# One engine table, rewritten: statistics of x for units 3 to 6 in the lead, x by gate weights behind the mix, expert weights remade in pieces

## The chip, the cores and the metric

The kernel runs on one core of a Trainium2 chip. The metric is device time in microseconds (us) of one execution. Before the change it was 300.04 us, the median of three runs (297.88 to 300.93).

## The reference, cut to what matters

The input is a batch of 16 images of 16 by 16 positions with 128 channels, 4096 tokens in all. Two blocks follow each other, both with a residual.

```python
# block 1, per image (n = 256 tokens)
q = xn @ Wq + bq;  k = xn @ Wk + bk;  v = xn @ Wv + bv      # xn = layernorm of x, 64 columns each
maps = softmax(k, axis=tokens);  vectors = softmax(v, axis=tokens)
desc = einsum('bnd,bnv->bvd', q, maps)
x = x + einsum('bvd,bnv->bnd', desc, vectors) @ Wr + br
# block 2, per token, 8 experts, the best two
t = layernorm(x);  logits = t @ Wg;  w = softmax(top2(logits))
h = t @ W1[e];  g = t @ W3[e] + b3[e];  x = x + sum_e w_e * (silu(h) * g) @ W2[e]     # F = 384
```

## The kernel before, in words

The tokens are worked on in eight units of four 128-token pieces (two images each). A written-out table of steps -3 to 8 (`iteration`, one for each engine, with the same step number i) sets the order of each engine's instructions; nothing is scheduled at run time, each engine runs its list in order and waits on semaphores. Step i does the middle of unit i, the front of units i+1 (`new`) and i+2 (`later`), and the back of unit i-1 (`old`).

The work of a unit, in the order in which it depends on itself: `stats_of_x` and `add_eps` (VectorE, `BN_STATS` and `BN_AGGR`), `rough_rstd` (ScalarE, logarithm and exponential), `find_shift` (VectorE, a Newton step), `normalise_x` (ScalarE), `transpose_xn`, `copy_xnt`, `project_kv` (TensorE, ScalarE, TensorE), `max_kv` (VectorE), `exp_kv` (ScalarE), `invert_sums`, `normalise_probs`, `transpose_probs`, `copy_pk`, `weigh_tokens`, `copy_xk`, `mix_channels` (TensorE, 64 by 136), `add_mix_bias` (VectorE), `spread_br` and `attend` (TensorE), `add_logits`, `choose_pair`, `add_x`, `stats_of_x1`, `choose_experts` (VectorE), then, in the next step, `rank` (TensorE), `scale_gap`, `exp_gap`, `weigh_and_place` (VectorE), `normalise_t` (ScalarE) and eight indirect DMAs by GpSimd, `scatter_rows`, that write each token's row once for each of its two experts into `sorted_rows` in HBM. The logits of the second block are the product of normalised x with a centred gate weight, `logits_of_x` (TensorE, eight small matmuls), scaled on VectorE (`scale_x_logits`), plus a part that `attend` gives in extra columns.

The up weights (W1 and W3) must be centred over the input rows and their layernorm's last row replaced, since the rows are scattered with 127 normalised values and a constant 1 as the last. `remake_up(e)` does this on TensorE: a product of `elim` with the raw weights for each of W1 and W3, and a third product that adds expert e's b3 as the last row. ScalarE rounds the result to the high part (`round_weights`), VectorE subtracts it for the low part (`split_up`), and the banks are free for the expert after next only then. Two experts are remade in a step, from -1 to 3.

From step 4 on, sorted rows are read back in 71 tiles of 128 rows, each with one expert: `turn` on each engine, at the places of `TURNS`: tile -1 (preparation only) at place 1 of step 4, and eight a step from step 5. A turn is transpose, up (W1 and W3, high and low parts, six matmuls of 384 columns), activation, three transposes, down (six matmuls), and an indirect DMA by GpSimd into `result_rows`. The first tile waits for a table that VectorE computes in step 3 (`share_rows`, `fill_slots`) and for the scatters of units 1 and 2. In steps 0 to 3 `keep_busy` puts matmuls of ones, with no use for the result, on TensorE (four and three in a step).

Tiles 38 to 70 come behind the steps. At the end the sync queue reads the results back (`load_results`, 256 KB each, two halves for each of eight units): `wait_tiles` first takes sixteen counts from a table, one register load and one wait after another, for the early table and then, behind the ten loads of units 0 to 4, for the second (`first_half`, L508). VectorE adds the halves and ScalarE's queue stores them.

The sync queue (SP) is in order, too: it loads x, the raw weights, pads and then each tile's rows.

## Time and profile before

| | |
|---|---|
| median of 3 runs | 300.04 us |
| the profiled execution | 299.36 us, span 297.6 us |
| TensorE busy | 251.1 us (84% of the span) |
| ScalarE busy | 169.3 us (57%) |
| VectorE busy | 164.6 us (55%) |
| GpSimd busy | 133.7 us (45%) |
| DMA | 28.32 MB, mean 95 GB/s |

The shares are averages over three stages: a lead without tiles (to about 88 us), tiles beside unit steps and then alone (to about 283), and a tail of reading, adding and storing. TensorE's ends are modelled, so start to start is the better measure of a group's length.

### The profile page before, as it was taken

The page shows a single profiled execution, that of the slowest core. Times are in us where ns is not written, and L with a number is a line of the kernel's source. Part 1 is how long each engine was busy: PE and PEld are TensorE (multiplying, and loading weights), DVE is VectorE, ACT ScalarE, POOL GpSimd, SP SyncE. Part 2 cuts the span into 40 slices and gives each one's busy share as a digit, 9 for nine tenths or more (in the row PEclk, how much of TensorE's full clock was granted, in tenths as well). Part 3 has the DMA queues.
Part 4 walks back from the last instruction along what each step waited for, and adds up shares of the span by engine and source line. Part 5 has one row for each costly group of instructions (what it writes and reads, how often), then busy time and mean ns, then how long its engine had stood idle before and what let it go on. Part 6 is the DMA issues. An engine that isn't in the chain of part 4 may idle for free.

```text
span 297.6 us, 6603 instructions
## 1 busy us (share of the span) xinstructions
PE 251.1 (84%) x1602; PEld 208.7 (70%) x1602; DVE 164.6 (55%) x766; ACT 169.3 (57%) x484; POOL 133.7 (45%) x150
## 2 busy tenths in 40 slices
PE   8769897979839997989998896699998999999700
PEld 3435454645438986969897795689998999999600
DVE  4471868686764764485555448247533434343735
ACT  2635256657537679658756854775565565655400
POOL 4000006373721762773477377357763534444510
PEclk9657999997978999997999999999999999999975
DMA  4769301110112420112331011333333222147186
GB/s 124 257 208 326 88 0 37 36 45 29 48 43 58 116 65 19 47 53 73 90 85 62 29 55 54 83 92 89 109 101 89 57 61 77 46 142 269 33 273 238
DMA packets 31735, 28.32 MB, mean 95 GB/s; under 512 B 5146, under 2 KB 29540, under 8 KB 31700
## 3 DMA queue, kind: packets, MB, share of 16 engines
q1 hardware_dynamic: 24608, 16.82, 20.1%
q0 software_dynamic: 4320, 8.92, 8.9%
q10 hardware_dynamic: 2772, 2.17, 2.3%
q8 instruction: 15, 0.25, 0.4%
q14 instruction: 20, 0.16, 0.2%
HBM read 15.89 MB, written 12.01 MB: 94 GB/s over the span
## 4 chain that ended last, share of the span: by engine, by line
PE 55%; DVE 16%; issue 8%; ACT 8%; DMA 5%; SPq 4%; POOL 2%; DVEq 0%; ACTq 0%; POOLq 0%
PE bank L706 12%; PE bank L696 7%; PE bank L680 6%; PE bank L682 6%; PE bank L681 6%; PE bank L675 2%; SPq L508 2%; POOL sorted_rows L1460 2%; PE bank L613 2%; PE bank L568 2%; PE bank L622 2%; DMA both<-result_rows 1%; PE bank L585 1%; ACT row_buf L898 1%; DVE stats L1080 1%
## 5 line engine op out<-in xcount | busy, mean ns | idle before, releaser
L1460 POOL DMA_INDIRECT sorted_rows<-row_buf,position x64 | 61.6, 963 | 87.7 <-ACT row_buf L898 49.7
L1467 POOL DMA_INDIRECT result_rows<-ys,xs x71 | 68.4, 963 | 62.6 <-ACT ys L944 47.1
L1334 DVE TENSOR_TENSOR xs_lo<-bank,xs_hi 128x128 fp32r<-128x128 f32 x71 | 20.7, 291 | 80.3 <-ACT xs_hi L927 79.7
L706 PE MATMUL bank<-w_down,act_t 128*128 x426 | 60.0, 278 | 1.5 <-ACT act_t L937 1.5
L944 ACT ACTIVATE ys<-bank,xs 128x128 f32<-128x128 f32 x71 | 26.0, 367 | 59.0 <-PE bank L706 58.9
L706 PEld LDWEIGHTS bank<-w_down,act_t 128*128 128x128 f32 x426 | 53.8, 194 | 1.9 <-issue 1.9
L680 PE MATMUL bank<-w_up,xs_hi 128*128 x142 | 54.6, 385 | 0.0
L682 PE MATMUL bank<-w_up,xs_hi 128*128 x142 | 48.4, 341 | 0.0
L681 PE MATMUL bank<-w_up,xs_lo 128*128 x142 | 48.3, 340 | 0.0
L696 PE MATMUL bank<-ident,act_rows 128*128 128x128 f32 x213 | 35.9, 278 | 8.1 <-ACT act_t L937 6.1
L1341 DVE TENSOR_TENSOR act_rows<-silu_h,bank 128x384 f32<-128x384 f32 x71 | 38.9, 548 | 4.9 <-ACT silu_h L932 1.4
L932 ACT ACTIVATE silu_h<-bank 128x384 f32<-128x384 f32 x71 | 35.3, 497 | 5.7 <-PE bank L682 5.7
L696 PEld LDWEIGHTS bank<-ident,act_rows 128*128 128x128 f32 x213 | 25.8, 142 | 13.9 <-issue 9.5
L937 ACT ACTIVATE act_t<-bank 128x384 f32<-128x384 f32 x71 | 34.3, 483 | 0.0
L680 PEld LDWEIGHTS bank<-w_up,xs_hi 128*128 128x128 f32 x142 | 27.5, 193 | 0.0
L681 PEld LDWEIGHTS bank<-w_up,xs_lo 128*128 128x128 f32 x142 | 27.4, 193 | 0.0
L675 PE MATMUL bank<-ident,xs 128*128 128x128 f32 x71 | 20.3, 285 | 8.2 <-DVE xs_lo L1334 4.8
L682 PEld LDWEIGHTS bank<-w_up,xs_hi 128*128 128x128 f32 x142 | 27.1, 191 | 0.0
L927 ACT ACTIVATE xs_hi<-bank 128x128 fp32r<-128x128 f32 x71 | 19.8, 278 | 0.0
L675 PEld LDWEIGHTS bank<-ident,xs 128*128 128x128 f32 x71 | 10.5, 147 | 9.7 <-DVE xs_lo L1334 6.0
L898 ACT ACTIVATE row_buf<-x_all,shift,rstd 128x254 f32<-128x254 f32 x32 | 16.5, 594 | 0.0
L668 PE MATMUL bank<-all_ones 128*128 128x512 bf16 x42 | 15.2, 510 | 1.1 <-DVE all_ones L1029 1.1
(184 smaller groups left out, 347.6 us busy)
## 6 DMA issues: line engine op xcount, KB each, us to landing
xs<-sorted_rows SPq DMA_DIRECT2D x71, 65.0 KB, 1.9
both<-result_rows SPq DMA_DIRECT2D x16, 256.0 KB, 4.4
x_all<-x_dram SPq DMA_DIRECT2D x8, 256.0 KB, 3.5
out_dram<-both ACTq DMA_DIRECT2D x8, 256.0 KB, 2.6
both<-L_ffn_W_dram SPq DMA_DIRECT2D x2, 960.0 KB, 8.4
w_down<-L_ffn_W_dram SPq DMA_DIRECT2D x3, 512.0 KB, 10.3
both<-L_ffn_W_dram SPq DMA_DIRECT2D x2, 576.0 KB, 5.9
result_rows<-ys,xs POOLq DMA_INDIRECT x71, 2.3
```

The source lines that it names most:

```text
L675: nc.tensor.transpose(rows_t_of(s), xs[s.ring][:, 0:P], ident[:]).then_inc(xst_ps, 1)
L680: nc.tensor.matmul(o, xs_hi[s.par][:], w[0], start=True, stop=False)
L681: nc.tensor.matmul(o, xs_lo[s.par][:], w[0], start=False, stop=False)
L682: nc.tensor.matmul(o, xs_hi[s.par][:], w[1], start=False, stop=True).then_inc((h_ps, g_ps)[j], 1)
L696: last = nc.tensor.transpose(act_t_of(s)[:, k * P:(k + 1) * P], act_rows[s.par][:, k * P:(k + 1) * P], ident[:])
L706: last = nc.tensor.matmul(bank[4][:, 0:C], act_t[s.par][:, k * P:(k + 1) * P], w_down[:, ds(e, 1), k * C:(k + 1) * C].rearrange("p a c -> ...
L932: nc.scalar.activation(silu_h[s.par][:], h_of(s), ACT.Silu).then_inc(silu_ready, 1)
L937: nc.scalar.activation(act_t[s.par][:], act_t_of(s), ACT.Copy).then_inc(act_t_ready, 1)
L944: nc.scalar.activation(ys[s.n % RESULTS][:], bank[4][:, 0:C], ACT.Copy, scale=xs[s.ring][:, WEIGHT:WEIGHT + 1]).then_inc(y_sb, 1)
L1341: nc.vector.tensor_tensor(act_rows[s.par][:], silu_h[s.par][:], g_of(s), ALU.mult).then_inc(act_ready, 1)
L1460: nc.gpsimd.indirect_dma_start(out=sorted_rows.ap(), out_offset=bass.IndirectOffsetOnAxis(ap=position[u.par][:, c:c + 1], axis=0), in_=row ...
L1467: nc.gpsimd.indirect_dma_start(out=result_rows.ap(), out_offset=bass.IndirectOffsetOnAxis(ap=xs[s.ring][:].bitcast(I32)[:, DEST:DEST + 1], ...
```

## The change

It does five things.

- Statistics. `stats` and `mean_var` have a place for each unit, so the waits of `mean_var_read` go. The statistics of x of unit 3 move to step -1, those of units 4, 5 and 6 to step 0; steps 1 to 3 have none.
- The logits of x, and their scaling on VectorE, move behind the mix, in all steps.
- The bias b3 no longer goes through TensorE. ScalarE rounds it, VectorE takes the low part, and the sync queue copies the rows (16 transfers of 1.5 KB, two for each expert behind its `split_up`) into row 127 of the up weights. TensorE waits for them before tile -1.
- An expert is remade in two halves that stand apart; `round_weights` and `split_up` of the step's earlier expert come earlier; in steps -1 to 3 `transpose_probs` of the next unit stands at the end of a step instead of the start of the next. Fillers go from step 0 and eight come into step -2.
- The sync queue fetches all counts of a table before the waits, and those of the second table before the early loads.

The core of the diff (left out: declarations of the new semaphores and buffers, and the pieces for steps -2 and -1):

```diff
+            sp.wait_ge(b3_hi_ready, 1)
+            sp.wait_ge(b3_lo_ready, 1)
+            for e in range(E):
+                sp.wait_ge(up_lo_ready, e + 1)
+                for half, part in enumerate((b3_hi, b3_lo)):
+                    sp.dma_start(w_up[:].bitcast(F32)[P - 1:P, e, 1, half, :],
+                                 part[:].bitcast(F32)[e:e + 1, :]).then_inc(b3_rows_in, 16)
...
             sp.wait_ge(half_table, 1)
-            wait_tiles(early_half)
+            wait_tiles(counts_of(early_half))
+            first_counts = counts_of(first_half)
             for u in range(EARLY_UNITS):
                 for k in range(K):
                     load_results(Slot(u, LAST_RING, NU), k)
-            wait_tiles(first_half)
+            wait_tiles(first_counts)
...
-            def remake_up(e):
+            def remake_up(e, j):
+                if j == 0:
+                    pe.wait_ge(early_in if e < LOADED_FIRST else late_in, EXPERT_LOADS)
+                    pe.wait_ge(elim_ready, 1)
+                    at_least(pe, up_lo_ready, e - 1)
+                last = nc.tensor.matmul(up_banks(e)[j][:, 0:F], elim[:], w_raw[:, e, j, :], start=True, stop=True)
+                if j == 1:
+                    last.then_inc(up_ps, 1)
...
                 turn(slot_of_turn(i, 0))
-                if exists(i):
+                if exists(i) and i.n >= FIRST_STEP:
                     transpose_probs(i)
                 if exists(old):
                     rank(old)
-                if exists(new):
-                    logits_of_x(new)
...
-                if warm_up:
-                    at_least(pe, up_lo_ready, 2 * i.n)
+                    keep_busy(5, bank[4])
+                if middle is not None and i.n > 0:
+                    at_least(pe, up_lo_ready, middle - 1)
                     keep_busy(4)
+                    remake_up(middle, 0)
                 turn(slot_of_turn(i, 2))
                 if exists(i):
                     mix_channels(i)
-                if warm_up:
+                if exists(new):
+                    logits_of_x(new)
+                if middle is not None and i.n > 0:
                     keep_busy(3)
+                    remake_up(middle, 1)
...
-                if middle is not None:
-                    remake_up(middle)
                 turn(slot_of_turn(i, 5))
                 if exists(later):
                     transpose_xn(later)
+                if exists(new) and new.n < FIRST_STEP:
+                    transpose_probs(new)
+                if i.n == -2:
+                    keep_busy(3, bank[4])
+                if i.n == 0:
+                    for j in range(2):
+                        remake_up(middle, j)
+                elif end is not None and i.n > 0:
+                    remake_up(end, 0)
...
                 if end is not None:
-                    remake_up(end)
+                    remake_up(end, 1)
... ScalarE
                 turn(slot_of_turn(i, 0))
+                if has_norms(later) and i.n < FIRST_STEP:
+                    rough_rstd(later)
                 if exists(i):
                     copy_pk(i)
...
                     copy_xk(i)
+                if before is not None:
+                    round_weights(before)
                 turn(slot_of_turn(i, 2))
                 if exists(old):
                     normalise_t(old)
-                if before is not None:
-                    round_weights(before)
... VectorE
                 turn(slot_of_turn(i, 1))
+                if i.n == 0:
+                    stats_of_x(Step(0, 4))
                 if exists(new):
+                    invert_sums(new)
+                turn(slot_of_turn(i, 2))
+                if exists(old):
+                    weigh_and_place(old)
+                if i.n == 0:
+                    stats_of_x(Step(0, 5))
+                    stats_of_x(Step(0, 6))
...
                 if exists(i):
                     add_mix_bias(i)
+                if i.n != -1 and exists(new):
+                    scale_x_logits(new)
                 turn(slot_of_turn(i, 4))
-                if i.n != -1 and exists(i.shift(3)):
+                if i.n < -1 or i.n == 4:
                     stats_of_x(i.shift(3))
+                if before is not None:
+                    split_up(before)
...
-                for e in (before, middle):
-                    if e is not None:
-                        split_up(e)
+                if middle is not None:
+                    split_up(middle)
```

The order on TensorE in step 1, before (transposes of unit 1's probabilities, rank of unit 0, logits of x of unit 2, weigh, fillers, mix, fillers, attend, and then experts 3 and 4 with unit 3's transposes and projection between them):

```order
L622 MATMUL bank<-wg_mid,xn_t 128x8 x4
L585 MATMUL bank<-pk,xn 128x64 x4
L668 MATMUL bank<-all_ones 128x512 x4
L595 MATMUL bank<-wqr,xk 64x136 x2
L668 MATMUL bank<-all_ones 128x512 x3
L605 MATMUL bank<-br_parts,ones_row 128x272 x2
L613 MATMUL bank<-mix,probs 128x136 x4
L660 MATMUL bank<-both,elim 128x384
L661 MATMUL bank<-both,elim 128x384
L662 MATMUL bank<-b_in,b_row 128x384
L563 MATMUL bank<-ident,xn 128x128 x4
L568 MATMUL bank<-xn_t,wkv 128x512
```

The same place now:

```order
L597 MATMUL bank<-pk,xn 128x64 x4
L678 MATMUL bank<-all_ones 128x512 x4
L670 MATMUL bank<-both,elim 128x384
L607 MATMUL bank<-wqr,xk 64x136 x2
L634 MATMUL bank<-wg_mid,xn_t 128x8 x4
L678 MATMUL bank<-all_ones 128x512 x3
L670 MATMUL bank<-both,elim 128x384
L617 MATMUL bank<-br_parts,ones_row 128x272 x2
L625 MATMUL bank<-mix,probs 128x136 x4
L575 MATMUL bank<-ident,xn 128x128 x4
L588 MATMUL bank<-ident,probs 128x64 x4
L670 MATMUL bank<-both,elim 128x384
```

The logits (L622, now L634) went from the front to behind the mix, expert 3 from behind attend to before it, and no product with b3 is left.

VectorE in step 0, from the shift of unit 2's norm on, before:

```order
L1108 SCALAR_TENSOR_TENSOR shift<-mean_var,rstd 128x8
L1151 TENSOR_TENSOR x_logits<-bank,std_x 128x32
L1138 RECIPROCAL inv_sum<-exp_sum 128x2
L1122 TENSOR_TENSOR mix<-bank,bqr 64x272
L1069 BN_STATS stats<-x_all 128x6 x4
L1074 BN_AGGR mean_var<-stats 128x2 x4
L1161 TENSOR_TENSOR logits<-bank,x_logits 128x16 x2
```

And now, where the statistics of units 4, 5 and 6 stand in front of the bias of the mix:

```order
L1138 SCALAR_TENSOR_TENSOR shift<-mean_var,rstd 128x8
L1099 BN_STATS stats<-x_all 128x6 x4
L1104 BN_AGGR mean_var<-stats 128x2 x4
L1168 RECIPROCAL inv_sum<-exp_sum 128x2
L1099 BN_STATS stats<-x_all 128x6 x4
L1104 BN_AGGR mean_var<-stats 128x2 x4
L1099 BN_STATS stats<-x_all 128x6 x4
L1104 BN_AGGR mean_var<-stats 128x2 x4
L1152 TENSOR_TENSOR mix<-bank,bqr 64x272
L1181 TENSOR_TENSOR x_logits<-bank,std_x 128x32
L1229 TENSOR_TENSOR w_up<-bank,w_up 128x384 x2
L1191 TENSOR_TENSOR logits<-bank,x_logits 128x16 x2
```

The split of expert 0 (L1229) came in front of the logits; before, it stood at the end of the step with expert 1's.

## Rows read from the trace of the kernel before

**Rows 1.** The page's part 4: the chain that ended last, shares of the span.

```profile
PE 55%; DVE 16%; issue 8%; ACT 8%; DMA 5%; SPq 4%; POOL 2%; DVEq 0%; ACTq 0%; POOLq 0%
```

**Rows 2.** Windows by stage: busy us of each engine, granted clock, DMA share, GB/s.

```profile
107.00:132.00 25.00, 22.91 (x170) 20.69 (x169) 13.90 (x68) 19.23 (x53) 13.93 (x15) 1.00 0.12 39
```

**Rows 3.** Timeline of step 2: start, us, engine, line, operation, idle before and its releaser.

```profile
50.80 1.94 DVE L1199 TENSOR_TENSOR w_up<-bank,w_up 128x384 fp32r<-128x384 f32 x4
...
51.95 0.88 PE L660 MATMUL bank<-both,elim 128*128 128x384 f32 x2 [0.96 <-DVE w_up L1199]
...
52.65 0.68 DVE L1130 TENSOR_REDUCE neg_max<-bank 128x2 f32<-128x512 f32 x1
...
54.78 1.04 PE L622 MATMUL bank<-wg_mid,xn_t 128*128 128x8 f32 x8
...
55.50 0.17 DVE L1100 SCALAR_TENSOR_TENSOR newton<-var_eps,rough 128x8 f32<-128x8 f32 x1 [1.84 <-ACT rough L918]
...
55.67 1.08 PE L585 MATMUL bank<-pk,xn 128*128 128x64 f32 x8
...
56.79 0.28 ACT L891 ACTIVATE xk<-bank 128x128 f32<-128x128 f32 x1
...
57.55 0.68 PE L595 MATMUL bank<-wqr,xk 128*64 128x136 f32 x4
...
58.97 0.87 DVE L1069 BATCH_NORM_STATS2 stats<-x_all 128x6 f32<-128x128 f32 x4
...
59.17 1.19 PE L613 MATMUL bank<-mix,probs 64*128 64x136 f32 x8
...
60.43 0.26 DVE L1161 TENSOR_TENSOR logits<-bank,x_logits 128x16 f32<-128x16 f32 x2
...
64.90 1.94 DVE L1199 TENSOR_TENSOR w_up<-bank,w_up 128x384 fp32r<-128x384 f32 x4
```

**Rows 4.** Timeline of step 3 and the first tile.

```profile
71.07 2.06 ACT L898 ACTIVATE row_buf<-x_all,shift,rstd 128x254 f32<-128x254 f32 x4
...
83.39 1.94 DVE L1199 TENSOR_TENSOR w_up<-bank,w_up 128x384 fp32r<-128x384 f32 x4
...
88.07 0.45 PE L675 MATMUL bank<-ident,xs 128*128 128x128 f32 x1 [3.37 <-DMA xs<-sorted_rows]
```

**Rows 5.** The page's slices of 7.44 us: granted clock of TensorE in tenths.

```profile
PEclk9657999997978999997999999999999999999975
```

**Rows 6.** Windows, as rows 2: one microsecond of step 3.

```profile
71.00:72.00 1.00, 1.00 (x5) 0.22 (x4) 0.90 (x7) 1.00 (x3) 0.00 (x0) 0.67 0.00 0
```

**Rows 7.** Timeline of steps -2 to 0.

```profile
10.18 2.08 PE L568 MATMUL bank<-xn_t,wkv 128*128 128x512 f32 x2 [0.69 <-ACT xn_t L864]
...
17.11 0.91 ACT L878 ACTIVATE probs<-exps,inv_sum 128x256 f32<-128x256 f32 x2 [0.72 <-DVE inv_sum L1138]
...
20.09 0.30 ACT L850 ACTIVATE br_hi<-br_row 2x136 fp32r<-2x136 f32 x1
...
32.27 0.26 DVE L1161 TENSOR_TENSOR logits<-bank,x_logits 128x16 f32<-128x16 f32 x2 [0.54 <-PE bank L613]
```

**Rows 8.** Timeline, the start of step 5.

```profile
113.80 0.52 PE L696 MATMUL bank<-ident,act_rows 128*128 128x128 f32 x3 [1.55 <-ACT act_t L937]
```

**Rows 9.** Line L508: duration ns min/median/max, first and last start.

```profile
L508 SPq TENSOR_LOAD <-early_half x16: 263/267/274, 253.3 to 262.6; - x16
...
L508 SPq TENSOR_LOAD <-first_half x16: 261/270/809, 268.4 to 285.9; - x16
```

**Rows 10.** Chain of waits in the tail: start, us, what.

```profile
273.72 3.17 DMA result_rows<-ys,xs
...
289.71 4.45 DMA both<-result_rows
```

**Rows 11.** Timeline in the tail: last scatter, last loads of results.

```profile
283.80 1.04 POOL L1467 DMA_INDIRECT result_rows<-ys,xs  x1 [0.76 <-ACT ys L944]
...
286.57 3.60 SPq L502 DMA_DIRECT2D both<-result_rows  x6
```

88 lines of the change are left out of this document (46 added, 42 removed).

## The prediction

> **What bounds the kernel now.** I read the chain of waits first: TensorE carries 55% of it, VectorE 16%, and the sync queue 4% with one line, L508, that computes nothing [rows 1]. Then the windows by stage. From unit step 4 on, TensorE is busy 22.91 of 25 us at full clock [rows 2], so a tile starts when TensorE gets to it, and whatever the stage in front (the lead) saves reaches the end, less what is added to TensorE later. The three places to price are the lead, the tile steps 4 to 6, and the tail. All times are us from the span's start in the profiled execution: span 297.6, its own time 299.36, against a median of 300.04.
>
> **The lead, steps 1 to 3.** In the timeline of step 2 [rows 3] the reader is to see a ring: VectorE splits two experts (50.80), TensorE may then remake the next one (51.95, idle 0.96 before it), and only behind these matmuls stand the next transposes of probabilities, so that ScalarE's rough inverse and VectorE's Newton step come at 55.50, the copy of xk at 56.79, the mix at 57.55, attend at 59.17, the logits at 60.43 and the next split at 64.90. Split to split is 14.10. The change cuts the ring open: transposes and norms stand before the remaking, the bias matmuls are gone, the remade halves go between other work. The new ring, from the split: one expert only, half of 1.94, 0.97; maximum and bias of the next unit 1.0 (0.68 in its row and the short one behind it); from the Newton step to the end of the xk copy 1.57 (55.50 to 56.79 and its 0.28); 0.1 to the mix: 3.65. From mix to the end of attend it was 2.81 (57.55 to 59.17 + 1.19); now the logits of x, 0.89 (54.78 to the next start at 55.67), and one half of a remade expert, 0.75 (its row has 0.88, with a modelled end), stand in between: 4.45. From there to the next split VectorE does what it did, 4.54 (60.36 to 64.90). Together 12.64, so 1.46 less per step. TensorE's other work of a step (weigh, four fillers, a half in front of the mix; transposes, half, projection, half behind attend, some 3.5) still ends about 1 us before the ring closes. The statistics of x, 1.46 (58.97 to 60.43), leave VectorE in a stretch where it then waits for attend anyway, so they count nothing here; what they cost comes in step 0. For two rings, steps 1 and 2, I take **-2.8**, between -1.0 (a low clock for a few us) and -3.2.
>
> Step 3 hands over to the tiles through GpSimd: the first tile waits for the eight scatters of unit 2, which start after normalise_t [rows 4]. That was at 71.07, 6.17 behind the split at 64.90. Now it comes behind the xk copy (3.55) and one rounding of 0.85: 4.4. The scatters and the load until 88.07 are the same: **-1.75**. In front of the load stand sixteen small transfers of b3 rows on the same sync queue, the last two waiting for expert 7's split, which ended at 85.33 [rows 4]. One pair less before it and a ring without the low clock put it about 1 us before the last scatter lands; if it is late, that costs up to 1.0, and I keep that for the range.
>
> **The lead, steps -1 and 0.** This is the part with no row of its own. The first split and the first logits (32.27) hang on br_hi (20.09) [rows 7]. The probabilities come up to 2.9 earlier than 17.11, since their inverse stood behind statistics and waits; but the product that br_hi needs now follows the projection, and the projection took 2.08 at the low clock [rows 5, 7], so br_hi stays at about 20.1. Behind it VectorE now has split 0.9, b3's low part 0.4 (both estimates from instructions of like size), statistics of unit 3 1.46, maximum and bias 1.0, Newton 0.9, statistics of 4, 5 and 6 4.4, the mix bias 0.45, x logits and a split 1.1: 30.8 to 31.1 for the first logits, instead of 32.27. I take **-1.0**. One end is -2.4 (at full clock the projection, and so the product, would come about 1 us earlier, and the product itself is shorter); the other is +1.2, TensorE late with the remade experts 1 and 2 because step 0 has lost its seven fillers.
>
> **Tile steps 4 to 6.** The 0.89 of logits stood in step 4 in an idle stretch that lasts until 88.07 anyway [rows 4], and in step 5 inside ScalarE's block of two table loads, behind which TensorE idles 1.55 [rows 8]. Behind the mix there is nothing that they cover: TensorE idles 0.9 longer and then works 0.9 longer. Three steps of 0.89 are **+2.7**; the low end is 0, since the clock fell behind the stretch of small matmuls that they belong to, in step 3 [rows 6], and splitting it may avoid one.
>
> **The tail.** L508 loads a count and waits, sixteen times [rows 9]. After the result at 273.72 landed (3.17 later, 276.9), the queue spends until 286.57 on fifteen loads of 0.27 and what goes with them, and six loads of results go out together, the last from 289.71, landing 4.45 later [rows 10, 11]. The change fetches the counts earlier: they take 16 times some 0.5, 8, in front of the ten early loads, so those go out by about 275 (from 253.3: 9 for the early counts, 8, 5), just inside the 276.9. Then three loads leave at about 279, and the other three when the last result is in: the scatter at 283.80 plus the same 3.17 is 287.0 [rows 10, 11], the last load at 287.9. 289.71 less that is -1.8; fewer loads in flight may land a little faster. **-2.0**, from -1.0 to -3.1. The Trainium skill (DMA: Bandwidth & Descriptors, Latency and other measured facts) gives a register load a floor of some 600 ns; the rows have 0.27. By the page's figure sixteen would be 9.6, an estimate, and the early loads would end behind 276.9 by about an us.
>
> Counted at nothing: the buffers of statistics (memory only), the removed preparation of b3_row on VectorE (it stood beside waits), the fillers of step -2 (TensorE waited for ScalarE there).
>
> **Sum.** -2.8 - 1.75 - 1.0 + 2.7 - 2.0 = -4.85. 299.36 less that is 294.5; the median stood 0.7 above the profiled execution and I add half of it: **294.9**.
>
> **The rivals.** *A, the logits cost nothing*: for it, the low clock behind the small matmuls and the fact that TensorE must wait for ScalarE in each step; against it, TensorE is the bound there [rows 2]. 294.9 - 2.7 = 292.2. *B, the lead gives half*: step 0 starts TensorE cold, VectorE's statistics hold back the mix, and the queue is late with b3: +1.2 instead of -1.0 at the start, -1.4 instead of -2.8 for the rings, 0.6 for the queue; 294.9 + 4.2 = 299.1. *C, slower*: the clock. The rows show that it falls within a microsecond in which TensorE was busy throughout (a mean of 0.67, so from 2.4 to 1.2 GHz in the middle of it) [rows 6], and at 10.18 it was at the lower level, where the projection took 2.08. Now nothing fills step 0, and TensorE waits there for VectorE's mix bias for several us. A ring wholly at 1.2 GHz takes up to 4.45 more, from mix to attend. Two such rings are 8.9, and the time is 303.8. It decides from little more than one of them: 300.04 less 294.9 is 5.1. Against it: between about 30 and 82 us the page shows the clock low in one stretch only [rows 5], and the new ring keeps its seven fillers. The Trainium skill (TensorE: Matmul & The Clock Gate, The HAM clock gate) says that "the default state is throttled, and activity releases the throttle"; that speaks for C in step 0, while the row at 71 us shows a fall without an idle stretch, which the sentence alone would not give. *D, the tail does nothing*, since the queue is late or the landing is set by other traffic: 294.9 + 2.0 = 296.9.
>
> **Chances.** Forecast 0.50, A 0.17, B 0.13, D 0.12, C 0.08. A measurement of this kernel tells about 1% (3 us) from no change, so faster means below 297.0. The forecast's own range, from the ends above, is 292 to 297.5; with A whole and most of B and D, 8 in 10 lie in 291.0 to 298.6. Faster: forecast 0.44, A 0.17, D 0.07, B 0.02: 0.70. Same: forecast 0.06, D 0.05, B 0.10, C in a mild form 0.02: 0.23. Slower: C 0.06, B 0.01: 0.07.
>
> **What would show it.** The step from split to split at 12.6 (if 14, the ring is not cut); the first logits of unit 0 near 31; the first tile's transpose about 5.5 earlier than 88.07; an idle of 2.4 instead of 1.55 before the act transposes of step 5; the six late loads of results in two groups of three, the first before 280. A granted clock of 0.5 over more than 3 us in steps 1 to 3 makes it wrong upwards; a distance from first tile to last matmul that has not grown by 2 to 3 us makes it wrong downwards.

## The result, and the profile after

The changed kernel takes **297.01 us** (median of 19 executions, 296.01 to 300.89) beside 300.40 for the kernel before on the same chips (19 executions, 297.60 to 303.12). The ratio is 0.994, 95% interval 0.991 to 0.997: 0.6% faster, about 1.8 us, less than the 1% that the prediction took as what can be told, and far from its 1.7% (5.1 us). The median lies in the forecast's range of 292 to 297.5; the forecast itself, 294.9, is below every execution.

The ratio compares undisturbed executions only, which is why it is nearer to one than the two medians are.

The profiled execution is one of the longer ones, 300.29 us, with a span of 298.5 against 297.6 before. It has to be read piece by piece. First the page: what bounds the kernel is what it was [rows 1], except that the sync queue's 4% has gone to 1%:

```profile
PE 57%; DVE 15%; ACT 10%; issue 8%; DMA 5%; POOL 2%; SPq 1%; DVEq 0%; ACTq 0%; POOLq 0%
```

**The start.** VectorE and TensorE in steps -1 and 0, the rows that answer to [rows 7] (start, us, engine, line, operation):

```profile
15.76 2.07 PE L580 MATMUL bank<-xn_t,wkv 128*128 128x512 f32 x2
...
24.77 0.79 PE L607 MATMUL bank<-wqr,xk 128*64 128x136 f32 x4 [2.02 <-ACT xk L914]
...
26.81 0.84 DVE L1099 BATCH_NORM_STATS2 stats<-x_all 128x6 f32<-128x128 f32 x4
28.20 0.45 DVE L1152 TENSOR_TENSOR mix<-bank,bqr 64x272 f32<-64x272 f32 x1
28.68 0.19 DVE L1181 TENSOR_TENSOR x_logits<-bank,std_x 128x32 f32<-128x32 f32 x1
28.79 1.01 DVE L1229 TENSOR_TENSOR w_up<-bank,w_up 128x384 fp32r<-128x384 f32 x2
...
29.68 2.17 PE L625 MATMUL bank<-mix,probs 64*128 64x136 f32 x8
...
31.89 0.26 DVE L1191 TENSOR_TENSOR logits<-bank,x_logits 128x16 f32<-128x16 f32 x2 [2.09 <-PE bank L625]
...
36.92 1.02 DVE L1229 TENSOR_TENSOR w_up<-bank,w_up 128x384 fp32r<-128x384 f32 x2 [0.53 <-ACT w_up L931]
```

The kernel before, in the same places (mix on TensorE, mix bias, first full split on VectorE):

```profile
28.62 1.17 PE L595 MATMUL bank<-wqr,xk 128*64 128x136 f32 x4
...
29.83 0.45 DVE L1122 TENSOR_TENSOR mix<-bank,bqr 64x272 f32<-64x272 f32 x1 [2.85 <-PE bank L595]
...
36.71 1.95 DVE L1199 TENSOR_TENSOR w_up<-bank,w_up 128x384 fp32r<-128x384 f32 x4
```

The mix comes at 24.77, nearly four us earlier than before. Most of that is lost behind it. VectorE has three statistics in front of the mix bias, which comes at 28.20, only 1.6 earlier. VectorE then finishes expert 0's split at 29.80 and idles 2.09 until attend is done: attend takes 2.17, where later steps have 1.19. From mix bias to logits it is 3.69, where it was 2.44. So the logits come at 31.89, 0.4 earlier than 32.27, and the split that starts the first ring at 36.92, 0.2 *later* than 36.71. The forecast had 1.0 earlier.

**The rings.** The splits of steps 2 and 3 on VectorE, which answer to [rows 3]:

```profile
49.40 1.01 DVE L1229 TENSOR_TENSOR w_up<-bank,w_up 128x384 fp32r<-128x384 f32 x2
...
61.58 1.01 DVE L1229 TENSOR_TENSOR w_up<-bank,w_up 128x384 fp32r<-128x384 f32 x2
```

36.92, 49.40, 61.58: rings of 12.48 and 12.18 where they were 14.09 and 14.10. From there the first tile's transpose, at 82.63 by the next row, comes 21.05 later, where it was 23.17 [rows 4].

```profile
82.63 0.45 PE L685 MATMUL bank<-ident,xs 128*128 128x128 f32 x1 [5.59 <-DMA xs<-sorted_rows]
```

The lead is 5.44 shorter; 5.55 was forecast. That the sum agrees is luck: the rings and the hand-over gave 1.1 more, the start 1.2 less. The prediction also named a sign for being wrong upwards, a granted clock of 0.5 over more than 3 us in steps 1 to 3. It came, from 73 to 86.6 us, behind the step's last projection and over the first tile; TensorE had little to do there, and the hand-over was not longer for it.

**Step 5.** TensorE's timeline, the rows that answer to [rows 8]:

```profile
105.73 1.00 PE L597 MATMUL bank<-pk,xn 128*128 128x64 f32 x8
109.18 0.52 PE L706 MATMUL bank<-ident,act_rows 128*128 128x128 f32 x3 [2.44 <-ACT act_t L964]
```

Windows over the same stretch (length, busy time of PE, PEld, DVE, ACT, POOL with the number of instructions, then the granted clock, DMA share, GB/s):

```profile
106.00:108.00 2.00, 0.73 (x7) 0.60 (x6) 0.63 (x5) 1.78 (x6) 0.00 (x0) 1.00 0.00 0
108.00:110.00 2.00, 0.82 (x8) 0.85 (x9) 0.39 (x2) 1.74 (x6) 0.20 (x1) 1.00 0.01 4
110.00:112.00 2.00, 2.00 (x11) 1.74 (x9) 0.44 (x2) 1.43 (x5) 1.20 (x2) 0.64 0.10 33
112.00:114.00 2.00, 2.00 (x9) 1.47 (x8) 1.82 (x10) 1.93 (x4) 0.52 (x1) 0.50 0.10 33
114.00:116.00 2.00, 2.00 (x11) 2.00 (x11) 0.42 (x3) 0.00 (x0) 0.73 (x1) 0.50 0.00 0
...
120.00:122.00 2.00, 2.00 (x13) 2.00 (x13) 0.61 (x2) 1.45 (x5) 1.54 (x2) 0.80 0.13 44
```

The idle time is 2.44 where it was 1.55, as forecast (2.4). Behind it the clock falls from 1.00 to 0.50 (from 2.4 to 1.2 GHz) and stays there until 121 us, with TensorE busy throughout. The number of instructions per window shows the price: 9 to 11 in 2 us, where [rows 2] has 170 in 25, 13.6 in 2.

**The tail.** The chain of waits (start, us, what), the rows that answer to [rows 10]:

```profile
285.53 3.31 DMA result_rows<-ys,xs
...
288.98 0.36 SPq L510
289.39 0.73 SPq L510
290.16 4.94 DMA both<-result_rows
```

The sync queue's register loads (duration in ns, first and last start), which answer to [rows 9]:

```profile
L514 SPq TENSOR_LOAD <-early_half x16: 261/266/287, 255.0 to 263.3; - x16
L514 SPq TENSOR_LOAD <-first_half x16: 261/268/358, 265.4 to 273.7; - x16
```

The register loads no longer stand in the late wait, and the chain goes through the last scatter instead. From that scatter to the last load's issue it is now 290.16 - 285.53 = 4.63, where it was 289.71 - 283.80 = 5.91 [rows 10, 11]: 1.3 saved. But the load takes 4.94 instead of 4.45.

The six late loads do leave in two groups of three, but the first group at 281.3 to 284.7 and not before 280: the sixteen counts hold up the ten early loads, which begin at 274.3, when those of the kernel before (from 263.2) had just landed. The early loads themselves are down by 286.3 and do not reach the last ones. What they push back is what hangs on them, the stores of the five early units: their last one landed at 288.9 before, 0.8 ahead of the last load's issue, and lands at 293.7 now, 3.5 behind it. The DMA queues from 290 to 293.7 us (q10 has the stores, q1 the loads; packets, MB, share of the 16 engines):

```profile
q10 hardware_dynamic: 602, 0.57, 60.5%
q1 hardware_dynamic: 558, 0.54, 41.7%
```

In the kernel before, from 289.7 to 294.2 us, q1 is alone:

```profile
q1 hardware_dynamic: 1187, 1.13, 74.0%
```

### The profile page after: what moved, and what is told of

It reads as the page before. It is cut to its first block, busy times and chain, and to the rows that moved or that the text cites. A ratio compares the mean times of both kernels' runs of the same rounds, so it can differ in the third digit from the quotient of the medians.

```text
span 298.5 us, 6585 instructions
## 1 busy us (share of the span) xinstructions
PE 245.3 (82%) x1587; PEld 210.4 (70%) x1587; DVE 164.1 (55%) x765; ACT 169.9 (57%) x485; POOL 133.8 (45%) x150
## 3 DMA queue, kind: packets, MB, share of 16 engines
q10 hardware_dynamic: 2772, 2.17, 2.4%
## 4 chain that ended last, share of the span: by engine, by line
PE 57%; DVE 15%; ACT 10%; issue 8%; DMA 5%; POOL 2%; SPq 1%; DVEq 0%; ACTq 0%; POOLq 0%
PE bank L716 14%; PE bank L706 7%; PE bank L692 7%; PE bank L690 7%; PE bank L691 7%; PE bank L625 3%; PE bank L685 3%; POOL sorted_rows L1504 2%; PE bank L634 2%; PE bank L670 2%; ACT act_t L964 2%; ACT L998 2%; DMA both<-result_rows 2%; PE bank L607 1%; DVE stats L1099 1%
## 5 line engine op out<-in xcount | busy, mean ns | idle before, releaser
L716 PEld LDWEIGHTS bank<-w_down,act_t 128*128 128x128 f32 x426 | 54.4, 196 | 1.9 <-issue 1.9
L690 PE MATMUL bank<-w_up,xs_hi 128*128 x142 | 55.0, 387 | 0.0
L692 PE MATMUL bank<-w_up,xs_hi 128*128 x142 | 49.1, 346 | 0.0
L691 PE MATMUL bank<-w_up,xs_lo 128*128 x142 | 48.9, 344 | 0.0
L1376 DVE TENSOR_TENSOR act_rows<-silu_h,bank 128x384 f32<-128x384 f32 x71 | 39.0, 549 | 4.8 <-ACT silu_h L959 1.4
L706 PEld LDWEIGHTS bank<-ident,act_rows 128*128 128x128 f32 x213 | 26.4, 144 | 16.3 <-issue 10.9
L954 ACT ACTIVATE xs_hi<-bank 128x128 fp32r<-128x128 f32 x71 | 19.7, 277 | 2.1 <-PE bank L685 2.1
L670 PE MATMUL bank<-both,elim 128*128 128x384 f32 x32 | 15.2, 579 | 0.0
```

The costliest lines, as they stand in the source:

```text
L690: nc.tensor.matmul(o, xs_hi[s.par][:], w[0], start=True, stop=False)
L691: nc.tensor.matmul(o, xs_lo[s.par][:], w[0], start=False, stop=False)
L692: nc.tensor.matmul(o, xs_hi[s.par][:], w[1], start=False, stop=True).then_inc((h_ps, g_ps)[j], 1)
L706: last = nc.tensor.transpose(act_t_of(s)[:, k * P:(k + 1) * P], act_rows[s.par][:, k * P:(k + 1) * P], ident[:])
L716: last = nc.tensor.matmul(bank[4][:, 0:C], act_t[s.par][:, k * P:(k + 1) * P], w_down[:, ds(e, 1), k * C:(k + 1) * C].rearrange("p a c -> ...
L1376: nc.vector.tensor_tensor(act_rows[s.par][:], silu_h[s.par][:], g_of(s), ALU.mult).then_inc(act_ready, 1)
```

## The experiments

A common ruler makes the profiles comparable: the start of VectorE's gated rows (the product that writes act_rows, L1376; L1341 in the kernel before) of each of the 71 tiles, less that of the kernel before (92.23 for tile 0, 278.04 for tile 70). Where the difference changes, something was lost or won in that place. Step 4 ends with tile 1, step 5 has its logits at tile 9, step 6 at tile 17, step 7's idle time is ahead of tile 24. "Tail" is the span less the start of tile 70; it was 19.56. "Filled" and "products nobody reads" mean matmuls of ones on TensorE whose result is not used.

| run | tile 0 | tile 1 | tile 8 | tile 9 | tile 16 | tile 17 | tile 23 | tile 25 | tile 70 | tail | median us | ratio to before |
|---|---|---|---|---|---|---|---|---|---|---|---|---|
| the changed kernel | -5.33 | -4.69 | -4.22 | -0.30 | +0.57 | +1.26 | +1.31 | +1.32 | +1.73 | 18.73 | 297.01 | 0.994 |
| after_again | -4.35 | -3.30 | -3.22 | -2.55 | -2.75 | -2.05 | -1.98 | -0.63 | -0.10 | 19.06 | 297.32 | 0.995 |
| logits_front | -4.42 | -4.19 | -4.20 | -4.20 | -4.29 | -4.29 | -4.28 | -2.77 | -2.40 | 19.16 | 295.55 | 0.986 |
| fill_holes | -5.17 | -4.38 | -4.34 | -3.65 | -3.89 | -3.20 | -3.16 | -1.81 | -1.58 | 17.84 | 297.06 | 0.994 |
| before_behind | +0.23 | +1.25 | +1.29 | +1.97 | +1.79 | +2.47 | +2.50 | +3.86 | +4.21 | 19.35 | 305.22 | 1.020 |
| lead_only | -4.10 | -3.84 | -3.78 | -3.79 | -3.86 | -3.86 | -3.76 | -2.24 | -1.95 | 19.71 | 297.54 | 0.990 |
| tail_only | +4.37 | +4.41 | +4.41 | +4.41 | +4.37 | +4.38 | +4.38 | +5.82 | +5.72 | 18.64 | 299.17 | 0.995 |
| front_fill | -5.42 | -5.45 | -5.42 | -5.42 | -4.31 | -4.30 | -4.20 | -4.19 | -2.94 | 18.10 | 293.48 | 0.980 |
| front_first | -6.09 | -6.08 | -6.08 | -6.08 | -6.15 | -6.14 | -6.05 | -4.53 | -4.22 | 18.48 | 296.11 | 0.981 |
| best | -6.21 | -6.20 | -6.20 | -6.20 | -6.27 | -6.26 | -6.16 | -6.14 | -5.77 | 17.53 | 292.15 | 0.978 |
| best_stats | -5.94 | -5.93 | -5.93 | -5.93 | -5.01 | -5.01 | -4.89 | -4.87 | -3.72 | 18.38 | 292.49 | 0.978 |
| best_start | -8.12 | -8.11 | -8.07 | -8.07 | -8.14 | -8.13 | -8.05 | -8.03 | -7.74 | 18.00 | 289.88 | 0.970 |
| before_again | +0.14 | +0.14 | +0.14 | +0.13 | +0.15 | +0.16 | +0.15 | +0.17 | +0.23 | 19.23 | (one run: 299.24) | |
| after_start | -7.32 | -6.23 | -6.16 | -5.48 | -5.70 | -5.01 | -4.93 | -3.57 | -3.39 | 18.45 | 295.33 | 0.987 |
| best_twelve | -11.39 | -11.38 | -11.33 | -11.33 | -10.43 | -10.43 | -10.35 | -10.33 | -9.14 | 17.80 | 288.78 | 0.966 |

The 95% intervals of the ratios reach 0.003 to 0.007 to either side, for front_first 0.011. Four series were measured on four chips, with the kernel before beside each (medians 300.42 for the runs up to before_behind, 300.99 from lead_only to front_first, 302.08 from best to before_again, 299.49 for the last two), so across series the ratios are the better comparison.

**after_again**, the changed kernel unchanged.

> The changed kernel unchanged, beside the others on one chip. Its first profile (300.29 us) shows TensorE's clock at 0.50 from 112 to 120 us, in step 5, and its other times lie in two groups: 296.0 to 297.4 us where the mean granted clock is 0.920 or more, 298.8 to 300.9 us where it is 0.914 or less. Theory 1 (the holes): the low stretch in step 5 is what tells the groups apart. This profile then either shows the stretch again and a time near 300, or none there and a time near 296.5. Rival 2 (chance elsewhere): the slow group has its loss in another place each time, and a profile near 296.5 us can show the stretch in step 5 all the same. Median by both 296.5 to 298.

The profile gave neither outcome of theory 1: an execution of 298.78 us (span 297.0) with no low stretch in step 5. The median, 297.32, is in the range of both. Windows over the same idle time (2.44 again):

```profile
108.00:110.00 2.00, 0.13 (x2) 0.00 (x0) 0.13 (x1) 1.81 (x4) 0.00 (x0) 1.00 0.00 0
110.00:112.00 2.00, 1.43 (x12) 1.46 (x13) 0.83 (x3) 1.35 (x6) 0.81 (x1) 1.00 0.01 4
112.00:114.00 2.00, 2.00 (x15) 1.56 (x13) 0.84 (x4) 2.00 (x7) 1.11 (x2) 1.00 0.10 33
```

It lost 1.0 in the lead and 1.4 behind step 7's idle time instead. So the long stretch in step 5 is one form of a loss that comes in several places, as rival 2 has it.

**logits_front**, the logits of steps 4 to 6 where the kernel before has them (the same on VectorE for their scaling):

```diff
                 if exists(old):
                     rank(old)
+                if exists(new) and i.n >= FIRST_STEP:
+                    logits_of_x(new)
...
                 if exists(i):
                     mix_channels(i)
-                if exists(new):
+                if exists(new) and i.n < FIRST_STEP:
                     logits_of_x(new)
```

> The changed kernel with the logits of x (L634) of steps 4 to 6 back ahead of the first slot of the step on TensorE, and their scaling back on VectorE; the lead is left as changed. Theory 1: with the logits behind the mix TensorE idles 2.44 us in step 5 ahead of the act transposes, instead of 1.55, and the clock falls behind that hole in a part of the executions, which costs 3.9 to 4.5 us each time. With the logits in front the hole is 1.4 to 1.6 us, no stretch at 0.50 follows it, and the slow group is gone or rare: median 294.5 to 295.5 us (295.4 is the lower group's 296.4 less the 0.9 us of idle time). Rival 2: the logits' place is without effect on the clock and hides in the hole anyway: 296 to 298 us, with a low stretch in step 5 or 6 in as many executions as before.

295.55, the ratio 0.986 where the changed kernel's on the same chip is 0.995: the move costs the changed kernel about 2.6 us (1.8 by the two medians). The ruler shows it as the forecast had it, a fixed price per step without any fall of the clock: +0.67 from tile 8 to 9 and +0.70 from 16 to 17 in after_again, 0.00 and 0.00 here; step 4 costs 1.05 there and 0.23 here. The idle time in step 5 is back at 1.53. Rival 2, that the place costs nothing, is out.

**fill_holes**, products nobody reads ahead of the weighing of steps 5 and 6:

```diff
                 pe.wait_ge(pk_sb, u.n + 1)
+                for _ in range(FILL.get(u.n, 0)):       # FILL = {5: 20, 6: 12}
+                    nc.tensor.matmul(bank[1][:, 0:2 * P].rearrange("p (a b) -> p a b", a=2), all_ones[:],
+                                     all_ones[:].unsqueeze(1).broadcast_to([P, 2, P]), start=True, stop=True)
```

> The changed kernel with products nobody reads (256 columns each, 20 in step 5 and 12 in step 6) on TensorE ahead of the tokens' weighing, where it idled 2.44 us in step 5 and 1.4 in step 6. Theory 1: the idle time before the act transposes of step 5 falls below 0.5 us, nothing else is delayed by more than 0.3 us, and the clock stays at 1.00 through steps 5 and 6: median 296.0 to 296.8 us and no execution over 298. Rival 2: a fall comes anyway, in steps 5 to 6, since it is not set off by this hole: two groups as before, median 296.5 to 298. Rival 3 (it is the load itself, not the hole, that brings the clock down): the added work makes falls more frequent and the median 299 or more.

The idle time was filled (0.24 left), the steps 5 and 6 ran at 1.00, and the median is the changed kernel's. Theory 1 in its strong form, that the hole in step 5 makes the changed kernel's spread, has fallen: four of the twelve executions are over 298, one of them at 300.41, and the profile has its fall in step 7.

**before_behind**, the kernel before with the logits behind the mix in steps 4 to 6 alone (the edit of logits_front the other way round).

> The kernel before with one part of the change: the logits of x behind the mix in steps 4 to 6. Theory 1: the hole in step 5 grows from 1.55 to 2.4 us, so this is 0.9 us slower with nothing else, and in executions whose clock falls behind that hole another 4 us: median 1 to 4 us above the kernel before. Rival 2: at most 0.9 us slower, with no more low stretches than the kernel before. The prediction had +2.7 us for this part.

2.0% slower. Again +1.0, +0.68 and +0.68 at tiles 1, 9 and 17, 2.4 together, then 1.36 behind step 7's idle time, where this execution's clock fell and the two profiles of the kernel before have none. The ratio stands for 5.9 us, with an interval of 3.9 to 8.0, more than the 2.4 and a fall; the profiled execution, 303.42, is one of the faster of the six. What the rest is, is not shown.

**lead_only** and **tail_only** take the parts one by one. lead_only is logits_front with the old wait for the second table at the tail:

```diff
             wait_tiles(counts_of(early_half))
-            first_counts = counts_of(first_half)
...
-            wait_tiles(first_counts)
+            for b in range(RING):
+                count = sp.value_load(first_half[0:1, b:b + 1], min_val=16, max_val=16 * ((NS + RING - 1) // RING))
+                wait_in_front(sp, waited_sp, (y_out[b], count))
```

> The changed kernel with the logits of x of steps 4 to 6 in front again and with the counts of the last wait read where the kernel before reads them, so that the lead alone is changed. The run with the logits in front and the tail changed gave a median of 295.55 us and a ratio of 0.986 to the kernel before. Theory A (the tail is worth what the traces show between the last tile and the last load's start, 1.1 to 1.7 us, less 0.5 to 0.8 us that the last load then takes longer): 0.4 to 1.2 us slower than that run, 296.0 to 296.8 us. Rival B (the tail's forecast, 2.0 us, holds in most executions): 297.5 us. Against the kernel before, Theory A gives the lead 3.5 to 4.5 us of gain, the forecast had 5.55.

tail_only puts the new fetching of counts, for both tables, into the kernel before.

> The kernel before with the tail's part of the change alone: the counts of the last wait are loaded into SyncE's registers ahead of the first results' loads. From the last tile's gated rows to the start of the last load the kernel before took 11.67 us and the changed kernel 10.0 to 10.5. Theory A: the same 1.2 to 1.7 us here up to the load's start and a load 0.3 to 0.8 us longer than 4.45 us, 0.4 to 1.2 us faster than the kernel before in all. Rival B: 2.0 us faster, as forecast. Rival C: nothing, within 0.3 us.

By its median lead_only is at rival B's 297.5 (2.0 us above logits_front, but on another chip), by its ratio 1.2 above, the upper end of theory A, and the intervals of the two overlap. The column "tail" settles this term better: the four profiles with the old wait have 19.2 to 19.7 (mean 19.5), the twelve with the new one 17.5 to 19.2 (mean 18.35). The tail's part is worth **1.1 us**, not 2.0. tail_only's ratio, 0.995 with an interval from 0.989 to 1.000, agrees, though by itself it would not exclude rival C. lead_only's ratio gives the lead alone 2.9 us.

The twelve profiles with the new wait also show what makes the last load long. Sorted by what the stores moved while it was under way, from 0.14 MB (best) over 0.38 (fill_holes, best_start) and 0.68 (the changed kernel) to 0.85 MB (logits_front), it took 3.81, 4.42 and 4.35, 4.94 and 5.28 us. Without stores beside it, but with all six late loads under way together, it took 4.12 to 4.53 in the four profiles with the old wait.

tail_only also shows how far the old lead can stray. In its profile the clock was at 0.50 from 8.3 to 32.2 us, the first full split came at 39.36 and tile 0 was 4.37 late.

**front_fill**, logits_front with 10, 10 and 20 products ahead of the weighing of steps 5, 6 and 7.

> The changed kernel with the logits of x of steps 4 to 6 in front, and with products nobody reads (256 columns each: 10 in steps 5 and 6, 20 in step 7) on TensorE ahead of the tokens' weighing. Every kernel so far idles 2.44 us in step 7 ahead of the act transposes (before, at 164.75 us, too), and four of six profiles show the clock at 0.5 to 0.6 right behind it, which costs 1.4 us, and again in step 8 in three. Theory 1 (a fall of the clock needs a hole of 2 us or more before it): no fall in steps 5 to 7, median 1 to 1.5 us under the run with the logits in front alone (295.55), 294.0 to 294.6. Rival 2: falls come with or without the holes, within 0.5 us of 295.55. Rival 3: the added work brings more falls, and it is slower than 296.

293.48, 2.1 under logits_front by the medians and 1.8 by the ratios. Step 7 of logits_front, TensorE's timeline:

```profile
157.04 1.00 PE L597 MATMUL bank<-pk,xn 128*128 128x64 f32 x8
160.47 0.87 PE L706 MATMUL bank<-ident,act_rows 128*128 128x128 f32 x3 [2.44 <-ACT act_t L966]
```

Its windows there:

```profile
160.00:162.00 2.00, 1.53 (x8) 1.56 (x9) 0.75 (x2) 1.04 (x4) 0.95 (x1) 0.59 0.10 33
162.00:164.00 2.00, 2.00 (x9) 2.00 (x9) 0.00 (x0) 0.91 (x3) 0.18 (x1) 0.56 0.10 33
```

The same place with the idle time filled, in the run "best", which has the same fillers:

```profile
158.59 0.52 PE L710 MATMUL bank<-ident,act_rows 128*128 128x128 f32 x3 [0.29 <-ACT act_t L971]
```

And its windows:

```profile
160.00:162.00 2.00, 2.00 (x15) 1.56 (x14) 0.83 (x3) 2.00 (x7) 0.96 (x1) 1.00 0.14 41
162.00:164.00 2.00, 2.00 (x16) 1.74 (x15) 1.31 (x9) 2.00 (x7) 0.00 (x0) 1.00 0.10 33
```

Over all sixteen profiles: with step 7's idle time of 2.44 the clock fell at it (in its last 0.3 us, or up to 1 us behind it) in 8 of 11, with it filled in 0 of 5. In step 5 an idle time of 2.44 was followed by a fall in 1 of 4, a shorter one in 0 of 12. But front_fill itself has a fall in step 6, at 130.9 us, with no idle time over 0.9 in the 6 us before it; theory 1, which had no fall in steps 5 to 7, is wrong in that. Step 8 had a fall in 7 of the 11 and in 4 of the 5. So filling an idle time took away the falls at that place, and not every fall.

**front_first**, logits_front with 11 products (512 columns) in the slot where TensorE waits for the first tile, and **best**, both additions:

```diff
                     pe.wait_ge(up_lo_ready, E)
+                    keep_busy(11)
```

> The changed kernel with the logits of x of steps 4 to 6 in front, and with 11 products nobody reads (512 columns each) on TensorE in the 5.6 us in which it waits for the first tile's rows. All six profiles show the clock at 0.50 from before the first tile until 3.4 to 5 us after it, where the first tile's products take 0.52 us each instead of 0.33 and the weighing 1.81 instead of 1.00. Theory 1: held busy, TensorE runs the first tile at the full clock and everything behind it comes 1.5 to 2.2 us earlier: median 293.4 to 294.0. Rival 2: the clock is up again only after the first tile, and the products come late into its way: 0 to 1 us slower than 295.55.

> Both additions together on the changed kernel with the logits of x of steps 4 to 6 in front: 11 products nobody reads ahead of the first tile, and 10, 10 and 20 in steps 5, 6 and 7. Alone the first brought the first tile's gated rows 0.6 to 0.7 us earlier than the same kernel without it, the others took away the fall of the clock in step 7 (1.5 us). If the clock's falls are set off by the holes, the two add: median 292.5 to 293.3 us. If a fall that is avoided in one place comes in another instead, it is 293.5 to 295.

The clock is up by 83 us instead of 86 to 89, and the first gated rows come 0.7 to 0.8 earlier than the earliest without it; less than expected, since the first of the products run at 0.50 themselves. Neither expectation of front_first fits: theory 1 had 1.5 to 2.2 us at the first tile, and the median, 296.11, lies where rival 2 has it. Its six executions lie in two groups, three at 293.2 to 294.1 and three at 298.2 to 298.8, so its times do not tell what the products are worth; the 0.7 to 0.8 of the traces do. best is at 292.15, below each of its halves, though by the ratio only 0.7 us below front_fill, within the intervals. No fall came in its steps 5 to 8.

**best_stats** and **best_start** repair the start: the statistics of unit 6 go behind the mix bias and the split, and then products nobody reads come into steps -1 and 0.

```diff
                     stats_of_x(Step(0, 5))
-                    stats_of_x(Step(0, 6))
...
                 if before is not None:
                     split_up(before)
+                if i.n == 0:
+                    stats_of_x(Step(0, 6))
```

> The kernel of the run 'best' with the statistics of unit 6 in step 0 moved behind the mix bias, the logits' scaling and the split, so that one of the three statistics that the change put into step 0 no longer stands in front of the mix bias on VectorE. In all profiles of the changed kernel the mix was done at 25.7 us at the latest, and the mix bias came at 28.17, right behind the statistics of unit 6 (26.77 to 28.14). Theory S (the start's forecast gain was lost to the statistics ahead of the mix bias): the mix bias comes at 26.9 to 27.5, attend and the first logits 0.6 to 0.8 us earlier than 31.86, and so does the first tile; median 0.5 us lower. Rival L (it was lost to TensorE at the low clock, whose logits of x end at 27.4 to 27.9 and whose attend takes 2.18 instead of 1.19): at most 0.2 us, since the scaled logits are waited for too.

```diff
+                if i.n == 0:
+                    keep_busy(4)
                 if middle is not None and i.n > 0:
                     at_least(pe, up_lo_ready, middle - 1)
...
                 if exists(new):
                     logits_of_x(new)
+                if i.n == -1:
+                    keep_busy(5, bank[4])
+                if i.n == 0:
+                    keep_busy(3)
```

> The kernel of the run before this one, with products nobody reads (512 columns each) in steps -1 (5) and 0 (4 ahead of the mix, 3 behind the logits of x), where the kernel before had its 4 and 3 and the changed kernel none. All profiles of the changed kernel show the clock at 0.50 from 14 or 16 us to 34 or 37 us without a break; two profiles of the kernel before show it back at 1.00 from 22 to 26 us and from 30 us on. Rival L: the fillers bring the clock back before 30 us, attend takes 1.19 instead of 2.18, and the first logits come 0.8 to 1.2 us earlier; median 0.8 us lower. Theory S alone: nothing more to gain. The other way: the clock stays low and the fillers stand in the way at 0.43 us each: up to 0.7 us slower.

The mix bias and the first logits on VectorE, in best:

```profile
28.12 0.45 DVE L1159 TENSOR_TENSOR mix<-bank,bqr 64x272 f32<-64x272 f32 x1
...
31.81 0.26 DVE L1198 TENSOR_TENSOR logits<-bank,x_logits 128x16 f32<-128x16 f32 x2 [2.09 <-PE bank L629]
```

In best_stats:

```profile
27.01 0.44 DVE L1159 TENSOR_TENSOR mix<-bank,bqr 64x272 f32<-64x272 f32 x1
...
31.08 0.26 DVE L1198 TENSOR_TENSOR logits<-bank,x_logits 128x16 f32<-128x16 f32 x2 [0.79 <-PE bank L629]
```

In best_start:

```profile
25.28 0.44 DVE L1165 TENSOR_TENSOR mix<-bank,bqr 64x272 f32<-64x272 f32 x1
...
28.97 0.26 DVE L1204 TENSOR_TENSOR logits<-bank,x_logits 128x16 f32<-128x16 f32 x2 [0.79 <-PE bank L629]
```

The statistics alone are worth 0.73 at the logits (the median does not show it, 292.49 against 292.15), the fillers another 2.1. What the fillers do is in TensorE's rows of step -1. In best:

```profile
15.67 2.07 PE L581 MATMUL bank<-xn_t,wkv 128*128 128x512 f32 x2
```

In best_start:

```profile
12.59 1.24 PE L682 MATMUL bank<-all_ones 128*128 128x512 bf16 x5
...
15.60 1.12 PE L581 MATMUL bank<-xn_t,wkv 128*128 128x512 f32 x2
```

Five products, 1.24 us together, in an idle time of 1.34 keep the clock at 1.00 until 25.0 us, where it had fallen at 14.9. The projection takes 1.12 instead of 2.07, and so on through the product for br_hi and the remade expert. The gain is twice the expected 0.8 to 1.2 and came another way: the clock did fall at 25.0, attend still takes 2.18, and the mix bias is earlier because everything in front of it is.

**before_again**, one more profile of the kernel before.

> The kernel before unchanged, one look, for a third profile of its lead. Its two relatives with an unchanged lead had the first tile's gated rows at 92.46 and 96.60 us, its own first profile at 92.23, while all seven profiles with the changed lead lie between 86.1 and 88.1. If the old lead varies because of the clock in its rings, the first gated rows lie between 91 and 97 us here too, with a stretch at 0.50 between 50 and 80 us in the cases that are late. If 96.60 was an exception, it is at 92.2 to 92.5.

Tile 0 at 92.37: the old lead is at 92.2 to 92.5 in three profiles, and 96.60 in one. The start varies more: the first full split is at 35.25 (before_behind), 36.71, 36.75 and 39.36 (tail_only). A stretch at 0.50 between 50 and 80 us does not mark the late case: before_behind has one too, at 55.6 to 59.0.

**after_start**, the same repair of the start on the changed kernel and nothing else.

> The changed kernel with nothing else than the start mended: the statistics of unit 6 behind the mix bias, and the products nobody reads in steps -1 (5) and 0 (4 and 3). On the kernel with all other additions this brought the first logits from 31.81 to 28.97 us and the median from 292.2 to 289.9. The forecast of the change had -1.0 us for the start, and the profiles show +0.2 at the first split. If the start is a term of its own, this is 2 to 2.5 us faster than the changed kernel (297.0 and 297.3 in two series): 294.5 to 295.3. If most of the earlier gain came from a rarer fall of the clock later on, it is 296 or more. It keeps the hole of 2.44 us in step 5, so its profile is another throw for a fall there.

295.33, ratio 0.987: 1.7 to 2.0 us under the changed kernel by the medians, 2.2 to 2.5 by the ratios, and 2.0 to 3.0 at tile 0. The start is a term of its own. Steps 5 and 7 cost what they cost before (+0.68, +1.36).

**best_twelve**, twelve instead of four products ahead of the mix of step 0.

> The fastest kernel so far (289.9 us) with twelve instead of four products nobody reads ahead of the mix of step 0. There TensorE idled 1.81 us ahead of the mix at 23.12, the clock fell at 24.5, and attend, the transposes, the remaking and the projection behind it ran at 0.50 until 34 us. Eight more take 1.7 us at the full clock and fit into that idle time. If the fall needs the hole, the clock holds through step 0, attend takes 1.19 instead of 2.18, and the first tile comes 1.0 to 2.0 us earlier: median 288.0 to 289.0. If the clock falls anyway, the products take 0.43 us each in the mix's way: 0 to 1 us slower.

**288.78 us, ratio 0.966 (0.961 to 0.971), the lowest of the study** (best_start has 0.965 to 0.975, so the two intervals overlap). TensorE in step 0 of best_start:

```profile
23.12 0.68 PE L611 MATMUL bank<-wqr,xk 128*64 128x136 f32 x4 [1.81 <-ACT xk L927]
...
26.75 2.18 PE L629 MATMUL bank<-mix,probs 64*128 64x136 f32 x8
```

And of best_twelve:

```profile
20.17 2.75 PE L682 MATMUL bank<-all_ones 128*128 128x512 bf16 x12
23.01 0.68 PE L611 MATMUL bank<-wqr,xk 128*64 128x136 f32 x4
...
26.33 1.19 PE L629 MATMUL bank<-mix,probs 64*128 64x136 f32 x8
```

The mix is not later, the clock stays at 1.00 until 66 us, and tile 0 comes 3.3 earlier, more than expected. In the later part this execution has falls at 124.5 and 175.7 us, where best_start has a shorter one at 178.6 alone, and of the 3.3 only 1.4 are left at tile 70.

## Why the prediction was wrong

| term | forecast | first profile | after_again |
|---|---|---|---|
| rings of steps 1 and 2 | -2.8 | -3.5 | -3.1 |
| step 3 to the first tile | -1.75 | -2.1 | -2.1 |
| start, steps -1 and 0 | **-1.0** | **+0.2** | **+0.7** |
| logits behind the mix | +2.7 | +2.0 | +2.4 |
| tail | **-2.0** | **-0.8** | **-0.5** |
| falls of the clock behind the first tile | **none** | **+4.85** | **+1.7** |
| rest | 0 | +0.3 | +0.3 |
| sum | -4.85 | +0.9 | -0.6 |

The start is taken at the split that begins the first ring. The rows of logits are sums of the steps at tiles 1, 9 and 17; the falls are the rest of tiles 1 to 11 in the first profile (+5.5 less the 0.67 of step 5's logits), and of step 7 and 8 in the second.

- **Rings, hand-over, logits: right.** The ring was cut as described. Over nine profiles the first ring came out at 12.5 to 13.6 and the second at 12.1 to 12.2, where 12.64 was summed. The transfers of b3 rows on the sync queue cost nothing: the load of the first tile stood behind the last scatter. The logits' price was named with its mechanism and nearly its size, and logits_front and before_behind show it from both sides. Rival A (that they cost nothing) is out. This is the part of the change that should be taken back.
- **The start failed.** The step was "30.8 to 31.1 for the first logits". It added up VectorE's work and put the logits at its end. VectorE kept that sum, it was done with the split at 29.80. But attend stands between the mix bias and the logits, and was charged nothing: at a granted clock of 0.50 it made 3.69 us of what had been 2.44. With 2.44 the logits would have come at 30.64, an estimate, and that is the forecast. Between the logits and the next split 0.6 more was lost (5.03, before 4.44), on the way over the remade experts 1 and 2, whose rounding VectorE waited for. The text had this as its other end, +1.2, "TensorE late with the remade experts 1 and 2"; rival B has the same +1.2 as "step 0 starts TensorE cold", and rival C the clock as its cause. The rest of B did not come, nor did C's whole rings at 0.50.

  All nine profiles of the changed start without added products show the clock at 0.50 from 13.5 to 15.6 on, until 35.3 to 37.9 us. Four have no break in it and five one of some 3 us from about 22 on, so "without a break" in the text before best_start holds for four only. The kernel before was at that level too, from 8 to 11 us on [rows 5, 7]. Three of its four profiles came back to 1.00 at 21 to 24 us, before the fillers of its step 0 began (26.88 in the first profile), and again at 28 to 30; the fourth, tail_only, came back only at 32.2, although TensorE worked without a pause from 18.73. What the old fillers were worth is therefore not shown, and the +0.2 and +0.7 of the table stand against one profile of a start that itself spreads over 4.1 us. What is shown is that the forecast gain did not come, and that products nobody reads hold the level: in the three profiles with five of them in step -1 the clock stayed at 1.00 until 24.3, 25.0 and, with twelve more in step 0, 66.4, and the kernels with five are 2 to 3 us faster. The Trainium skill (TensorE: Matmul & The Clock Gate, The HAM clock gate) says "the default state is throttled, and activity releases the throttle". The trace agrees for step -1: five products in an idle time of 1.34 kept the projection at 1.12 instead of 2.07. The 13 us of work at 0.50 in tail_only is more than the sentence alone would give.
- **The tail was mis-sized.** The chain moved to the last scatter as forecast. Behind it stand 1.3 us of queue (4.63 less the 3.31 of the scatter's landing), where 0.9 was counted, and the last load took 4.94 instead of 4.45. The step that failed there is that ten early loads pushed back to 275 cost nothing. They went out from 274.3 to 279.1, later than counted, and the stores that hang on them then ran beside the last load, which took from 3.81 to 5.28 us the more of them it met. "Fewer loads in flight may land a little faster" left these stores out. The term is worth 1.1 over all profiles, between the forecast and rival D, whose second condition, a landing set by other traffic, came true in part. A register load took 0.27 us here too; the floor of some 600 ns that the Trainium skill (DMA: Bandwidth & Descriptors, Latency and other measured facts) gives did not show.
- **The falls behind the first tile were not priced.** The sum was made against a profile with none of cost in steps 7 and 8, and took for granted that the changed kernel would have none either. The idle time of 2.44 in step 7 was in that profile already, at 162.31 to 164.75 us, and the clock happened to hold. In 8 of 11 profiles it did not, at 1.4 to 1.5 us each. Kernels with the old lead pay this too (two profiles of four), so it should move the ratio little; the deeper idle time in step 5 is the changed kernel's own, and was followed by a fall of 4.85 us in one of four profiles. That the one caused the other there is argued and not shown: fill_holes took that idle time away and its median stayed where it was.

Taken together: start and tail account for 3.2 of the 4.3 us by which the profile of after_again missed the sum; a fall of the clock in step 7, which the profile of before was spared, and one in step 8 for another 1.7; what rings, hand-over and logits gave more, 1.0, goes the other way, and 0.3 are not assigned. Part of this is the profiled execution's own luck: it took 298.78 where its median was 297.32. Left open is why the clock falls in one execution of the same program and not in another, and what set off the falls in step 6 (five profiles; in front_fill behind idle times of 0.89 at most).

## What to carry to other kernels

Removing stand-in work from TensorE is an edit with a price: where an engine's next work is on the path, look up at which granted clock it would run without it, and price both levels. A sum made against one profiled execution carries that execution's luck with the clock; look at its long idle stretches (2.44 us here) and ask what a fall at each would cost. The same goes for the kernel that one compares with: its start alone spread over 4 us here. And a wait whose setup is fetched earlier only moves the queue's time: ask what then leaves later, and also what hangs on that (here the stores), and runs beside the last transfer.

## What the runs showed of the hardware that I had not expected

- The clock's fall and the idle time it goes with need not coincide. In step 7 it came 0.2 to 0.3 us *before* TensorE took up work again in four of the eight profiles with a fall (logits_front: work again at 160.47, and the windows above put the fall at 160.3), and 0.7 to 1.0 us *after* it in the other four. In the changed kernel's step 5 TensorE was idle until 109.18, the clock 1.00 up to 110, and 0.64 in the window to 112, in which it was busy throughout; in best_start it was idle until 23.12, and the clock fell at 25.0.
- A stretch at 0.50 lasted between about 3 us (step 7) and 10 us (step 5) where the tiles run, with TensorE busy for 82% of it or more, and up to 24 us in the start. The price of one fall where the tiles run was between nothing (step 8 in best_start, which loses no more from tile 25 to 70 than best without a fall) and 4.85 us.
- The last load of results took 3.81 us with 0.14 MB of stores beside it and 5.28 with 0.85 MB, with the same loads under way.
- Products nobody reads cost nothing where TensorE waited: twelve of 512 columns in the idle time ahead of step 0's mix left it at 23.01 (23.12 with four), and 20 of 256 columns, 2.36 us, took the idle time of step 5 from 2.44 to 0.24 with the transposes behind it in place.
